# A fused attention and low-rank Gelu layer, scheduled by hand: Gelu pairs spread over six steps, second products summed in SBUF, a third bank freed from them, row maxima transposed in one go

## The reference

```
x = x + attn(layernorm(x))     # 32 query heads, 16 key/value heads of 64, causal, ALiBi bias
P = layernorm(x) @ U1          # 256 -> 64
H = gelu(P @ V1 + b1)          # 64 -> 1024, tanh form
Q = H @ U2                     # 1024 -> 64
x = x + Q @ V2 + b2            # 64 -> 256
```

## Time and profile before

| | |
|---|---|
| median of 3 runs | 2898.99 us (2890.83, 2899.17, 2898.99) |
| the profiled execution | 2891.4 us, its span in the trace 2889.3 us |
| PE busy | 2700.1 us (93%) |
| ACT, POOL, DVE busy | 2206.9, 2013.4, 2012.7 us (76%, 70%, 70%) |
| one steady iteration | 174.3 us, of it PE busy 166.8 us |
| last iteration to its last exponentials | 49.9 us, then some 62 us of tail |

### The profile page before, as it was taken

How to read it: one execution, slowest core, us unless ns; L and a number is a source line. 1 busy time by engine, 2 the same in 40 slices (tenths; PEclk the granted TensorE clock), 3 DMA queues, 4 the chain that set the end, 5 groups by cost and what they waited for, 6 DMA issues and landing times.

```text
span 2889.3 us, 83994 instructions
## 1 busy us (share of the span) xinstructions
PE 2700.1 (93%) x31304; PEld 1851.9 (64%) x31304; DVE 2012.7 (70%) x6731; ACT 2206.9 (76%) x3892; POOL 2013.4 (70%) x1816
## 2 busy tenths in 40 slices
PE   4999999999999999999999999999999999999986
PEld 1676666766666666666766667666676766666663
DVE  7767677676766777676776777767677776776753
ACT  3777878777787877878778787777878778787782
POOL 1677777777777767777676777767777677776783
PEclk9999999999999999999999999999999999999997
DMA  6444344444444344443443434344343444434420
GB/s 172 99 96 91 89 91 79 104 88 91 86 88 99 82 94 90 86 97 79 104 90 90 89 87 97 84 96 87 86 98 80 100 90 89 93 77 102 88 60 22
DMA packets 491051, 260.83 MB, mean 90 GB/s; under 512 B 312842, under 2 KB 488970, under 8 KB 490378
## 3 DMA queue, kind: packets, MB, share of 16 engines
q1 hardware_dynamic: 490644, 255.46, 40.6%
HBM read 27.73 MB, written 8.39 MB: 12 GB/s over the span
## 4 chain that ended last, share of the span: by engine, by line
PE 72%; ACT 8%; DVE 7%; issue 7%; POOL 5%; SPq 1%; DMA 0%; DVEq 0%; ACTq 0%; POOLq 0%
PE proj L450 30%; PE scores L450 18%; PE o_acc L450 13%; PE max_scores L450 5%; PE ffn_acc L450 4%; POOL p_lo L1091 2%; DVE max_scores L931 2%; ACT h_f L831 2%; ACT p_hi L701 2%; POOL o_hi_lo L1099 2%; ACT p_f L742 2%; ACT L742 1%; DVE h_hi L1023 1%; POOL h_lo L1119 1%; ACT L831 1%
## 5 line engine op out<-in xcount | busy, mean ns | idle before, releaser
L1091 POOL TENSOR_TENSOR p_lo<-p_f,p_hi 128x512 f16<-128x512 f32 x1280 | 1475.8, 1160 | 571.2 <-ACT p_hi L701 571.0
L742 ACT ACTIVATE p_f<-scores 128x512 f32<-128x512 f32 x1280 | 756.4, 591 | 131.9 <-PE scores L450 128.1
L701 ACT ACTIVATE p_hi<-p_f 128x512 f16<-128x512 f32 x1280 | 800.4, 625 | 14.8
L931 DVE CUSTOM_DVE_ANT_0 max_scores<-max_scores,causal 128x384 f32<-128x384 f32 (+3 forms) x1184 | 562.9, 507 | 265.3 <-PE max_scores L450 254.7
L450 PE MATMUL scores<-q_hi_lo,k_lo_hi 128*128 128x512 f16 (+3 forms) x2048 | 613.6, 300 | 0.2 <-ACT p_f L742 0.2
L450 PE MATMUL scores<-q_hi_aug,k_hi_aug 128*128 128x512 f16 (+3 forms) x2048 | 586.3, 299 | 0.0
L450 PE MATMUL o_acc<-v_hi_one,p_lo 128*128 128x65 f16 x5120 | 519.4, 195 | 42.7 <-POOL p_lo L1091 39.7
L450 PEld LDWEIGHTS o_acc<-v_hi_one,p_lo 128*128 128x128 f16 x5120 | 471.5, 98 | 91.1 <-POOL p_lo L1091 62.6
L450 PE MATMUL o_acc<-v_hi_one,p_hi 128*128 128x65 f16 x5120 | 518.7, 194 | 0.0
L450 PE MATMUL o_acc<-v_lo,p_hi 128*128 128x64 f16 x5120 | 518.3, 193 | 0.0
L450 PEld LDWEIGHTS o_acc<-v_lo,p_hi 128*128 128x128 f16 x5120 | 469.3, 99 | 36.9 <-issue 0.6
(11 more groups left out here) (108 smaller groups left out, 4761.7 us busy)
## 6 DMA issues: line engine op xcount, KB each, us to landing
q_hi_aug<-q_pair_hi SPq DMA_DIRECT2D x512, 64.0 KB, 2.0
q_hi_lo<-q_pair_hi SPq DMA_DIRECT2D x512, 64.0 KB, 2.0
q_hi_lo<-q_pair_lo SPq DMA_DIRECT2D x512, 64.0 KB, 2.0
k_hi_aug<-k_pair_hi SPq DMA_DIRECT2D x256, 64.0 KB, 2.0
k_lo_hi<-k_pair_hi SPq DMA_DIRECT2D x256, 64.0 KB, 2.0
k_lo_hi<-k_pair_lo SPq DMA_DIRECT2D x256, 64.0 KB, 2.0
x_rows<-in_L_attn_inputs SPq DMA_DIRECT2D x17, 512.0 KB, 4.1
x_acc<-in_L_attn_inputs SPq DMA_DIRECT2D x64, 128.0 KB, 2.4
```

Source lines behind the costliest of these rows:

```text
L701: return nc.scalar.activation(out_ap, in_ap, ACT.Copy, scale=scale)
L742: nc.scalar.activation(p_f[:, k % 3, :], score_bank[k % 2][:, :], ACT.Exp).then_inc(exp_done, 1)
L931: last = nc.vector.tensor_tensor_reduce(out=bank, in0=bank, in1=causal[:, (T - 1 - qt) * P:S], scale=1.0, scalar=-3e38, op0=ALU.add, op1=A ...
L1091: nc.gpsimd.tensor_tensor(p_lo[:, slot, n, :], p_f[:, k % 3, :], p_hi[:, slot, n, :], ALU.subtract).then_inc(lo_p, 1)
```

## The change

It does three things. The Gelu pairs move from four places in steps 13 and 14 to one place in each of the steps 13, 15 and, in the next iteration, 1 and 3. The casts and `h_lo` of a pair stand one segment later, the second products one step and two segments later, and the end of the FFN (scale, split, `ffn_y`, the store) in step 5 of the next iteration. A short extra iteration (`TAIL`, steps 0 to 5) ends the last batch.

The second products of a pair go to a rotating projection bank, and DVE adds them up in SBUF in `q_sum`: one copy and three additions per batch. The bank `ffn_acc` becomes the second bank of the maxima at all times. The rotation now has 76 uses per iteration instead of 72.

The row maxima of a group of four heads are laid out as 32 columns, so that one PE transpose takes them all, where four of 8 columns did. ACT and DVE then split 32 x 128 instead of 8 x 512.

`q_lag` is 1 at all steps; in steps 13 to 15 it was 0, so there the low part of q stands one segment later on DVE.

```diff
-FFN_PAIRS = {(13, 1): 0, (13, 3): 1, (14, 0): 2, (14, 2): 3}
-
-U2_PAIRS = {(13, 4): 0, (14, 0): 1, (14, 2): 2, (14, 4): 3}
-U2_START = 13 * SEG + 4
-
-QF_AT, Y_AT = (15, 1), (15, 4)
+H_PAIRS = {(13, 1): 0, (15, 1): 1, (1, 1): 2, (3, 1): 3}
+
+SPLIT_PAIRS = {(13, 2): 0, (15, 2): 1, (1, 2): 2, (3, 2): 3}
+
+U2_PAIRS = {(14, 3): 0, (0, 3): 1, (2, 3): 2, (4, 3): 3}
+
+QF_AT, Y_AT, STORE_AT = (5, 0), (5, 1), 5
...
 def q_lag(s):
-    return 0 if s >= 13 else 1
+    return 1
...
         def max_place(s, n):
...
-            return (ffn_bank if in_ffn_bank(k) else max_bank), back
+            return max_bank[(SEG * s + n) % 2], 2
...
-                    for qt in range(T):
-                        last = nc.tensor.transpose(bank[0:8, qt * P:(qt + 1) * P], mcol[:, (s - 6) // 4 % 2, qt, :], ident[:, :])
-                    last.then_inc(pe_m, 1)
+                    nc.tensor.transpose(bank[0:8 * T, 0:P], mcol[:, (s - 6) // 4 % 2, :, :].rearrange("p c t -> p (c t)"),
+                                        ident[:, :]).then_inc(pe_m, 1)
...
-                def ffn_u2(pair):
+                def ffn_u2(f, pair):
+                    bank = next_proj(("u", pair), u_acc, f * 4 + pair + 1)
                     for c in (2 * pair, 2 * pair + 1):
...
+                        pe.wait_ge(hi_h, at(f * FC + c + 1))
+                        mm(bank[:, :], u2s[:, c, :], h_hi[:, c % 2, :], c % 2 == 0, False)
+                        pe.wait_ge(lo_h, at(f * FC + c + 1 + FREE))
+                        mm(bank[:, :], u2s[:, c, :], h_lo[:, c % 2, :], False, c % 2 == 1).then_inc(pe_u2, 1)
...
+                        if (s, n) in U2_PAIRS and ffn_in(i, s):
+                            f, pair = ffn_batch(i, s), U2_PAIRS[s, n]
+                            dve.wait_ge(pe_u2, at(f * FC + 2 * pair + 2))
+                            if pair == 0:
+
+                                dve.wait_ge(lo_qf, at(f + FREE))
+                                nc.vector.tensor_copy(q_sum[:, :], proj("u", 0)[:, :]).then_inc(u_acc, 1)
+                            else:
+                                dve.wait_ge(u_acc, at(f * 4 + pair))
+                                nc.vector.tensor_tensor(q_sum[:, :], proj("u", pair)[:, :], q_sum[:, :],
+                                                        ALU.add).then_inc(u_acc, 1)
```

More of the change, by code:

```diff
@@ L148, with steps @@
 PROJ = {use: k % BANKS for k, use in enumerate(projection_order())}
-FFN_USES = ("ln2", "p", "h", "y")
-def last_uses(b):
-    mine = [use for use in projection_order() if PROJ[use] == b]
-    steady = [use for use in mine if use[0] not in FFN_USES]
-    return {mine[-1], steady[-1]}
 MULTIPLES = (1, 2, 4, 8, 16, 32, 64, 80, 128, 192)
 FREE = 1
-FIRST, MID, LAST = "first", "mid", "last"
+FIRST, MID, LAST, TAIL = "first", "mid", "last", "tail"
+def steps(mode):
+    return range(STORE_AT + 1) if mode == TAIL else range(KV)
 class Count:
@@ L378, in body @@
             def body(i, mode):
-                for s in range(KV):
+                for s in steps(mode):
                     g = i * KV + s
```

198 lines of the change are left out of this document (92 added, 106 removed).

## The result

The changed kernel takes 2903.67 us (median of 10 runs, 2901.2 to 2904.4), the kernel before 2896.04 us (10 runs, 2890.83 to 2899.17): ratio 1.0028, 95% interval 1.0019 to 1.0037. It is slower, but within the 0.3% that the prediction called no change. The forecast was +15 us on the median and +18 us on the span; measured are +7.6 us and, in the profiled executions, 2902.2 for 2889.3 us, +12.9. The profiled execution of the kernel before (2891.4 us) is among its fastest, so the spans lie further apart than the medians.

A forecast was written before the change was run, and what follows sets the result against it. PE, busy 93%, bounds the kernel. A steady iteration's terms sum to +0.64 us, fourteen to +9.0; with -7.1 (iteration 1), -0.7 (first), +9.0 (last) and +7.9 (tail), +18 on the span. Forecast 2914 us, range 2874 to 2936.

The forecast's parts named there:

- Second bank of maxima: -5.10 us an iteration: Steps 13 to 15: all PE idle time, mostly waits for DVE's row maxima, goes, 5.10 us an iteration.
- POOL late: +1.85: After the pairs, mainly (14, 1): PE waits for POOL's late `p_lo`, 1.85 us an iteration, between 1.4 and 2.3.
- Exponentials late: +1.95: Steps 13, 1 and 3: PE waits some 0.65 us each for exponentials behind ACT's Gelu block, 1.95 an iteration.
- Output projection of step 15: +2.15: At (15, 4): PE waits 2.15 us for the bank of q, which DVE splits only after `xn_t_lo`.
- Y: At (5, 1): `ffn_y` waits for DVE's split behind ACT's scaling copy, +0.45 us an iteration, bounds nothing and 0.6.
- Additions at 0: End of segment 3 on DVE: four additions into SBUF of some 0.7 us fit where it otherwise waits, costing 0.
- The last iteration: +9.0: Steps 1 and 3 get pairs without projections to cover them, 3.85 us each, and y 1.3: +9.0 us.
- the tail: +7.9: End of program: each pair becomes a chain of 5.4 us, and the last SBUF addition adds 0.7: +7.9 us.
- The first iteration: -0.7: Start of the program: the first iteration saves two places of transposes, -0.7 us.
- (1): Rival: step 15's output projection doesn't wait, so 2882 us; with the case that ACT's block hides elsewhere too, chance 0.27.
- (2): Rival: the ends cost little, the last iteration absorbing its pairs (+0 to +3); some 2900 us, within 0.3%; chance 0.20.
- (3): Rival: Q's split, reading two SBUF operands, waits for a POOL instruction of 1.15 us each time; +17 us, 2931; chance 0.11.

The follow-up runs named there:

- Kernel 12: Changed kernel with q split ahead of x in step 15, altered bank rotations, Gelu pairs in steps 0 to 3, Y at (5,2): 2892.92 us, ratio 0.9996.
- kernel 3: Changed kernel with Gelu pairs, second products, Q and Y back at their old segments in steps 13 to 15: 2891.27 us, ratio 0.9991.

## Why the prediction was wrong

It gave a slower kernel 0.53 and the case that came, within 0.3%, 0.20. The medians moved in the forecast direction, by half of what was said.

**The step that failed is the first term, "Second bank of maxima: -5.10 us an iteration".** It was mis-sized, because it took PE's idle rows for the whole cost of the waits. Worked out from the windows: steps 13 to 15 took 42.89 us and take 34.92. Of the 7.97, 5.6 are work that went elsewhere (two pairs of h, three u, y, at the prediction's 0.86 and 1.3), 0.33 a transpose. New waits came in, with 0.16 for what each row hides: 0.48 at (13, 4), 0.16 at the q product ahead of it (too short to show in a row), 1.34 at (14, 1), 2.08 at (15, 4), 0.16 at the q product of (15, 2), together 4.22. So 7.97 - 5.6 - 0.33 + 4.22 = **6.26 us of waits went, where 5.10 were counted**. Over fifteen iterations that is 17 us. The missing 1.16 us are as much as seven waits hide at 0.16 each; the rows name five, so that two more must have been too short to show, which is inferred and not seen. Kernel 12 checks the size another way: its steps 13 to 15 have no pair and no idle time and take 9.45 + 8.24 + 10.34 = 28.03 us; with four h, four u, y and the longer transposes (8.5 us) they make 36.5, and the kernel before took 42.89, so that some 6.4 us were waits. The term's cause was wrong too: one bank at the new places costs 0.74, two banks at the old places gain nothing (there with q one segment later). It is the spreading that took most of the waits away.

**"POOL late: +1.85" was over-sized by 0.5.** Its lower bound, 1.3 at (14, 1) and nothing at (4, 1), is what came (1.18 in the row, 1.34 by the starts). The port conflict that I added for the upper bound is there, but small: the casts ran ahead, both in 0.76 us, and `p_lo` took 1.40 us instead of 1.16. Taking the middle between the ends was the mistake; the order of starts spoke for the lower one.

```profile
650.26 0.76 DVE L1004 CAST h_hi<-h_f 128x512 f16<-128x512 f32 x2
650.63 1.40 POOL L1083 TENSOR_TENSOR p_lo<-p_f,p_hi 128x512 f16<-128x512 f32 x1 [2.42 <-ACT p_hi L678]
```

By the Trainium skill (SBUF — State Buffer, "Who interferes with whom") when DVE is in a two-port mode, the engine that issues first has the shared ports for its whole instruction. When `p_lo` starts, at 650.63, 0.39 us of the casts are left (until 651.02), so the rule allows no more than that here, and the 0.24 us do not speak against it.

**"Exponentials late: +1.95" held**: 0.64 at each of three places, 0.48 at the scores and 0.16 ahead of them at the q product. **"Output projection of step 15: +2.15" held** (2.08), and so did **Y** (+0.54 for 0.45) and **the transposes** (-0.66, exactly, in the kernel that has them alone). **Additions at 0** held in the steady state; in the tail some 4 us (kernel 3) are put down to them, for which I had 0.7. Small waits that no row shows I had not seen: (0, 1) takes 3.07 us in the changed kernel (505.40 to 508.47) where it took 2.91 (507.98 to 510.89).

With the measured sizes the sum closes: -6.26 - 0.66 + 1.92 + 1.34 + 2.08 + 0.54 = -1.04 us, and three waits of 0.16 to 0.18 us (at (15, 2), at (0, 1), and in step 4, which takes 9.16 us where 8.12 and a u product of 0.86 make 8.98) bring it to -0.5, which is what a steady iteration gained.

**"The last iteration: +9.0"** came out as 13.0, and **"the tail: +7.9"** as 9.2. In the last iteration I priced two blocks and y as a chain on POOL. The windows split the 13.0: PE is idle 5.6 us longer (the waits for `p_lo` are 9.4 us for 7.8, and 3.7 for exponentials are new) and busy 7.4 us longer. By the prediction's own 0.86 and 1.3, two pairs of h, three u and y are 5.6 of the busy time, of which the sum named only y; the rest is about what the clock costs, which is 0.50 from 2809.8 to 2813.2. In the tail the clock is 0.64 for 0.73, and PE is busy 40.1 us for 35.6 with one matmul fewer; how much of the +9.2 that is, these runs don't tell. **"The first iteration: -0.7"** stays open within the scatter of the start.

The rivals: (1) "doesn't wait" is refuted, since it waits its 2.08 us. But its price of 32 us for that wait was wrong as well: taking the wait away gave 13 to 15 us, because the x half and a shared bank are late next. (2) "the ends cost little" is refuted, although its time came near: the ends cost more than forecast, and the steady state less. (3) did not come in the steady iterations: the split of Q, from two SBUF operands, took DVE 0.69 us at 562.99, what one from PSUM takes. But there POOL has nothing to do until 563.55, as the prediction said, so this doesn't test the conflict itself. In the last iteration the split starts while POOL's `p_lo` runs (2817.78 to 2818.94), and takes 1.06 us:

```profile
2818.43 1.06 DVE L837 SCALAR_TENSOR_TENSOR h_lo<-ffn_q_sum,h_hi 128x512 f16<-128x512 f32 x1 [1.21 <-ACT h_hi L678]
```

So the conflict shows once, and elsewhere the order of starts kept it away.

## What to carry to other kernels

Price a wait by the starts of the instructions on both sides of it against the same place without the wait, and not by its idle row: on PE each row was 0.16 us short here, and with seven waits an iteration that was larger than the effect looked for. When a stall goes, ask what was due just behind it: of the 2.08 us of one wait 0.6 came back in an iteration, and a second bank at the old places removed a wait and no time. Functions of different activation tables belong together, since two loads of 1.28 us frame each group, and a block on ACT is felt at every engine that needs its next result.
